# A recurrent kernel on TensorE: input and output projections as three float32r products of halves in place of six bf16 products, with the work of the steps rearranged

## What is computed

```python
# layer 0: a modulated linear layer; ys, d depend on cond only
ys = cond * scale
d = rsqrt(einsum('bi,io->bo', ys * ys, weight * weight) + EPS)
x = x + einsum('bsi,io->bso', x * ys[:, None, :], weight) * d[:, None, :]
# layer 1: a recurrent layer of 256 hidden units over the 256 steps, h0 = cond
Xz, Xr, Xh = X @ Wxz.T + bxz, X @ Wxr.T + bxr, X @ Wxh.T + bxh
def step(H, xs):
    xz, xr, xh = xs
    Z = sigmoid(xz + H @ Whz.T + bhz)
    R = sigmoid(xr + H @ Whr.T + bhr)
    H_tilda = tanh(xh + R * H @ Whh.T + bhh)
    H_new = Z * H + (1.0 - Z) * H_tilda
    return H_new, H_new @ Whq.T + bhq
x = x + scan(step, h0, ...)
```

## Time and profile before

| what | us |
| --- | --- |
| median of 3 runs | 640.48 (639.31 to 640.96) |
| the profiled execution | 639.56 |
| its span, first to last instruction | 637.8 |
| outside its span | 1.76 |
| start of step 0 | 22.5 |

### The profile page before, as it was taken

The page is one execution under the profiler, slowest core; times in us unless marked ns, Lnnn a source line. Parts: engine busy times, 40 slices in busy tenths (PEclk is TensorE's granted clock), DMA queues, the critical chain, the costliest instruction groups (busy, mean ns, idle before and its releaser), DMA issues.

```text
span 637.8 us, 39807 instructions
## 1 busy us (share of the span) xinstructions
PE 626.3 (98%) x16890; PEld 568.1 (89%) x16890; DVE 491.6 (77%) x4051; ACT 209.1 (33%) x1607; POOL 4.5 (1%) x11
## 2 busy tenths in 40 slices
PE   8999999999999999999999999999999999999987
PEld 3689999999999999999999999999999999999976
DVE  5789777777877778777877877777777777877776
ACT  3133333333233333333333333333333333333332
POOL 2000000000000000000000000000000000000000
PEclk9955555555555555555555555555555555555555
DMA  7000000000000000000000000000000000000000
GB/s 264 2 5 3 4 13 4 13 4 12 4 5 12 5 12 4 12 5 4 13 4 13 4 5 12 5 12 5 12 5 4 12 4 13 4 13 4 4 12 12
DMA packets 7174, 8.86 MB, mean 14 GB/s; under 512 B 1618, under 2 KB 5458, under 8 KB 6996
## 3 DMA queue, kind: packets, MB, share of 16 engines
q1 hardware_dynamic: 6416, 6.03, 2.9%
q10 hardware_dynamic: 580, 0.28, 0.2%
HBM read 4.21 MB, written 2.10 MB: 10 GB/s over the span
## 4 chain that ended last, share of the span: by engine, by line
PE 93%; DVE 4%; ACT 1%; DMA 1%; issue 1%; DVEq 0%
PE chunk_bank L670 53%; PE z_rec_bank L670 13%; PE chunk_bank L647 12%; PE y_bank L632 6%; PE z_bank L647 6%; PE chunk_bank L679 1%; DMA x<-x_cm 1%; PE chunk_bank L584 1%; DVE lin L383 1%; DVE r_hidden L517 1%; DVE hidden L563 1%; DVE r_hidden L521 0%; DVE r_hidden L525 0%; ACT scan_mul L327 0%; DVE xs L376 0%
## 5 line engine op out<-in xcount | busy, mean ns | idle before, releaser
L670 PE MATMUL chunk_bank<-r_hidden,w_part 128*128 128x8 bf16 x6144 | 206.2, 169 | 0.2
L670 PEld LDWEIGHTS chunk_bank<-r_hidden,w_part 128*128 128x128 bf16 x6144 | 184.7, 105 | 17.9 <-issue 0.6
L670 PEld LDWEIGHTS chunk_bank<-hidden,w_part 128*128 128x128 bf16 x3072 | 102.5, 104 | 34.5 <-DVE hidden L563 6.2
L670 PE MATMUL chunk_bank<-hidden,w_part 128*128 128x8 bf16 x3072 | 125.1, 173 | 4.5 <-DVE hidden L563 4.0
L563 DVE TENSOR_TENSOR_SCAN hidden<-scan_mul,hidden 128x24 f32<-128x24 f32 x512 | 80.7, 199 | 60.0 <-ACT hidden L330 53.8
L327 ACT ACTIVATE scan_mul<-z_pre 128x16 f32<-128x16 f32 x256 | 57.2, 223 | 197.1 <-DVE z_pre L529 197.1
L670 PE MATMUL z_rec_bank<-hidden_parts,w_part 128*128 128x24 bf16 x3072 | 121.5, 181 | 0.1
L670 PE MATMUL chunk_bank<-hidden_parts,w_part 128*128 128x8 bf16 x3072 | 119.3, 168 | 0.0
L325 ACT ACTIVATE r_bank<-chunk_bank 128x8 f32<-128x8 f32 x256 | 41.5, 162 | 212.1 <-PE chunk_bank L670 206.6
L670 PEld LDWEIGHTS z_rec_bank<-hidden_parts,w_part 128*128 128x128 bf16 x3072 | 103.2, 104 | 0.2 <-DVE z_rec_bank L465 0.2
L670 PEld LDWEIGHTS chunk_bank<-hidden_parts,w_part 128*128 128x128 bf16 x3072 | 102.9, 104 | 0.0
(11 more groups left out here) (86 smaller groups left out, 667.3 us busy)
## 6 DMA issues: line engine op xcount, KB each, us to landing
x<-x_cm SPq DMA_DIRECT2D x4, 512.0 KB, 7.9
out_cm<-result SPq DMA_DIRECT2D x15, 128.0 KB, 2.1
w_rec<-w_rec_cm SPq DMA_DIRECT2D x1, 768.0 KB, 8.2
w_in<-w_in_cm SPq DMA_DIRECT2D x1, 768.0 KB, 9.8
w_mod<-w_mod_cm ACTq DMA_DIRECT2D x1, 256.0 KB, 5.7
w_out<-w_out_cm SPq DMA_DIRECT2D x1, 256.0 KB, 10.3
out_cm<-result SPq DMA_DIRECT2D x1, 64.0 KB, 2.9
out_cm<-result SPq DMA_DIRECT2D x2, 32.0 KB, 1.9
```

The source lines that it names most:

```text
L670: return nc.tensor.matmul(cols, w_part[wp][:, gate, k, m * P:(m + 1) * P], moving, start=first, stop=True, skip_group_check=True)
```

## The change

- The input projections of blocks 2 to 15 and the output projections of blocks 1 to 14, six bf16 products per tile pair before, become three products of float32r operands (`HALVES`): high half of the weights by high half of the data, low by high, high by low. One is issued in the first slot, two in the second. A float32r tile has 4 bytes an element; a VectorE copy to it makes the high half, and a subtraction the low half.
- x1 (128 columns per block and chunk), the input weights, the output weights and now also the hidden states of a block (`h_hi`, `h_lo`, new) are split in this way. The copy stands where a subtraction stood; the halves of the hidden states are new instructions in steps 0 to 3 of blocks 2 to 15, after `z_pre`. The output weights' bf16 parts, which the products at the end still use, are split in block 2, steps 8 to 11.
- The order within a block: from block 1 on the input projection for Z is in steps 0 to 3, the output projection in steps 4 to 7, R and G stay in 8 to 11 and 12 to 15. Accordingly the single f32 products of block 1 stand in steps 4 to 7, the Z bias (`take_z`) in steps 4 and 5, `finish` in 8 and 9, and the bank that R's second half is written to follows.

```diff
-        x1_rest, x1_rest2 = (sb(name, [P, 2, KC, BC]) for name in ("x1_rest", "x1_rest2"))
-        w_in, w_in_rest, w_in_rest2 = (sb(name, [P, 3, KC, C]) for name in ("w_in", "w_in_rest", "w_in_rest2"))
+        x1_hi, x1_lo = (sb(name, [P, 2, KC, BC], fp32r) for name in ("x1_hi", "x1_lo"))
+        h_hi, h_lo = (sb(name, [P, KC, BC], fp32r) for name in ("h_hi", "h_lo"))
+        w_in = sb("w_in", [P, 3, KC, C])
+        w_in_hi, w_in_lo = (sb(name, [P, 3, KC, C], fp32r) for name in ("w_in_hi", "w_in_lo"))
+        w_out_hi, w_out_lo = (sb(name, [P, KC, C], fp32r) for name in ("w_out_hi", "w_out_lo"))
...
-            return n == 0 or (n == 1 and j < 4)
+            return n == 0 or (n == 1 and 4 <= j < 8)
...
+            def first_x1_half(n, k):
+                nc.vector.tensor_copy(x1_hi[:, n % 2, k, :], x1[:, k, n * BC:(n + 1) * BC]).then_inc(x1_hi_ready, 1)
+            def second_x1_half(n, k):
+                dve.wait_ge(x1_hi_ready, KC * (n - 2) + k + 1)
+                nc.vector.tensor_tensor(x1_lo[:, n % 2, k, :], x1[:, k, n * BC:(n + 1) * BC],
+                                        x1_hi[:, n % 2, k, :].bitcast(fp32), ALU.subtract).then_inc(x1_parts, 1)
...
+            def first_h_half(n, k):
+                nc.vector.tensor_copy(h_hi[:, k, :].rearrange("p (s b) -> p s b", b=B), steps_of_h(k, n)
+                                      ).then_inc(h_hi_ready, 1)
+            def second_h_half(n, k):
+                dve.wait_ge(h_hi_ready, KC * (n - 1) + k + 1)
+                nc.vector.tensor_tensor(
+                    h_lo[:, k, :].rearrange("p (s b) -> p s b", b=B), steps_of_h(k, n),
+                    h_hi[:, k, :].bitcast(fp32).rearrange("p (s b) -> p s b", b=B), ALU.subtract
+                ).then_inc(h_halves, 1)
...
+                if n == 2 and 8 <= j < 12:
+                    weight_split(j % 2, 1 + (j - 8) // 2)
...
-                if n > 0 and j in (4, 5):
-                    finish(n - 1, j - 4)
+                if n > 1 and j < 4:
+                    (first_h_half, second_h_half)[j % 2](n - 1, j // 2)
+                if n > 0 and j in (8, 9):
+                    finish(n - 1, j - 8)
...
+            HALVES = ((0, 0), (1, 0), (0, 1))
+            SLOTS_OF = (slice(0, 1), slice(1, len(HALVES)))
...
+                    for i in range(len(HALVES))[SLOTS_OF[slot]]:
+                        wp, part = HALVES[i]
+                        mm = nc.tensor.matmul(pre(1 - p, task, m, 0, BLOCK), (w_in_hi, w_in_lo)[wp][:, task, k, cols],
+                                              (x1_hi, x1_lo)[part][:, (n + 1) % 2, k, :], start=(j == 0 and i == 0),
+                                              stop=True, skip_group_check=True)
...
-                bulk(n, j, slice(0, 1))
+                bulk(n, j, 0)
...
-                bulk(n, j, slice(1, len(PRODUCTS)))
+                bulk(n, j, 1)
```

More of the change, by code:

```diff
@@ L43, in modulated_linear_then_gru @@
     bf16 = mybir.dt.bfloat16
+    fp32r = mybir.dt.float32r
     ALU = mybir.AluOpType
@@ L159, in r_gate @@
         def r_gate(k, n, j):
-            bank = r_bank if k == 0 else (z_bank if n > 0 and j < 4 else y_bank)
+            bank = r_bank if k == 0 else (z_bank if n > 0 and 4 <= j < 8 else y_bank)
             return bank[:, KC * BC:KC * BC + B]
@@ L195, in modulated_linear_then_gru @@
         weight_parts = sem("weight_parts")
-        x1_rest_ready = sem("x1_rest_ready")
+        x1_hi_ready = sem("x1_hi_ready")
         x1_parts = sem("x1_parts")
+        h_hi_ready = sem("h_hi_ready")
+        h_halves = sem("h_halves")
+        weight_hi = sem("weight_hi")
+        weight_halves = sem("weight_halves")
         gates_seeded = sem("gates_seeded")
@@ L397, in take_z, with steps_of_h @@
                                         z_bank[:, m * BC:(m + 1) * BC], bias_z[:, m:m + 1], None, ALU.add)
[L399 to L409, removed]
+            def first_x1_half(n, k):
[4 more added lines that the diff above has]
+                                        x1_hi[:, n % 2, k, :].bitcast(fp32), ALU.subtract).then_inc(x1_parts, 1)
+            def steps_of_h(k, n):
+                return h_word(k, slice(n % 2 * BLOCK, (n % 2 + 1) * BLOCK))
+            def first_h_half(n, k):
[7 more added lines that the diff above has]
+                ).then_inc(h_halves, 1)
             def add_x(k, cols):
@@ L471, in _, with weight_halves_of, weight_split @@
             dve.wait_ge(scan_set, 1)
-            def weight_split(i, part):
-                w, rest, rest2 = (w_in, w_in_rest, w_in_rest2) if i < 3 * KC else (w_out, w_out_rest, w_out_rest2)
+            def weight_halves_of(i, part):
+                w, hi, lo = (w_in, w_in_hi, w_in_lo) if i < 3 * KC else (w_out, w_out_hi, w_out_lo)
                 at = (i // KC, i % KC) if i < 3 * KC else (i - 3 * KC,)
-                w, rest, rest2 = (a[(slice(None),) + at + (slice(None),)] for a in (w, rest, rest2))
+                w, hi, lo = (a[(slice(None),) + at + (slice(None),)] for a in (w, hi, lo))
+                if part == 1:
+                    nc.vector.tensor_copy(hi, w).then_inc(weight_hi, 1)
+                else:
+                    dve.wait_ge(weight_hi, i + 1)
+                    nc.vector.tensor_tensor(lo, w, hi.bitcast(fp32), ALU.subtract).then_inc(weight_halves, 1)
+            def weight_split(k, part):
+                w, rest, rest2 = (a[:, k, :] for a in (w_out, w_out_rest, w_out_rest2))
                 if part == 1:
@@ L480, in weight_split @@
                 else:
-                    dve.wait_ge(weight_rest, i + 1)
+                    dve.wait_ge(weight_rest, k + 1)
                     nc.vector.tensor_tensor(rest2, rest, high(rest), ALU.subtract).then_inc(weight_parts, 1)
@@ L509, in _ @@
                         dve.wait_ge(ld_win, 16)
-                    weight_split((j - 4) % 6, 1 + (j - 4) // 6)
+                    weight_halves_of((j - 4) % 6, 1 + (j - 4) // 6)
                 if n == 1 and 4 <= j < 8:
@@ L513, in _ @@
                         dve.wait_ge(ld_wout, 16)
-                    weight_split(6 + j % 2, 1 + (j - 4) // 2)
+                    weight_halves_of(6 + j % 2, 1 + (j - 4) // 2)
+                if n == 2 and 8 <= j < 12:
+                    weight_split(j % 2, 1 + (j - 8) // 2)
                 for k in range(KC):
@@ L532, in _ @@
                     axis=mybir.AxisListType.X, op=ALU.add).then_inc(pre_z, 1)
-                if n > 0 and j in (4, 5):
-                    finish(n - 1, j - 4)
-                if n + 1 < NB and j in (8, 9):
-                    if j == 8:
+                if n > 1 and j < 4:
+                    (first_h_half, second_h_half)[j % 2](n - 1, j // 2)
+                if n > 0 and j in (8, 9):
+                    finish(n - 1, j - 8)
+                z_at = 8 if n == 0 else 4
+                if n + 1 < NB and j in (z_at, z_at + 1):
+                    if j == z_at:
                         dve.wait_ge(z_ready, n + 1)
-                    take_z(1 - p, j - 8)
+                    take_z(1 - p, j - z_at)
                 if n == LAST and j in (14, 15):
@@ L556, in _ @@
                             dve.wait_ge(x1_ready, x1_count(n + 2))
-                        first_x1_rest(n + 2, j - 12)
+                        first_x1_half(n + 2, j - 12)
                     if j in (14, 15):
-                        second_x1_rest(n + 2, j - 14)
+                        second_x1_half(n + 2, j - 14)
                 for k in range(KC):
@@ L595, in _, with bulk @@
             PRODUCTS = ((0, 0), (1, 0), (2, 0), (0, 1), (1, 1), (0, 2))
-            W_IN = [high(w[:, :, :, :]) for w in (w_in, w_in_rest, w_in_rest2)]
             W_OUT = [high(w[:, :, :]) for w in (w_out, w_out_rest, w_out_rest2)]
[L599 to L605, removed]
+            HALVES = ((0, 0), (1, 0), (0, 1))
+            SLOTS_OF = (slice(0, 1), slice(1, len(HALVES)))
+            def bulk(n, j, slot):
                 p = n % 2
@@ L609, in bulk @@
                 cols = slice(m * P, (m + 1) * P)
-                last = some.stop == len(PRODUCTS)
+                if n == 0:
+                    task = (None, Z, R, G)[j // 4]
+                else:
+                    task = (Z, "out", R, G)[j // 4]
                 if whole_bulk(n, j):
-                    if last and j >= 4:
+                    if slot == 1 and task == "out":
+                        if j == 4:
+                            pe.wait_ge(ld_wout, 16)
+                        mm = out_tile(1 - p, m, k)
+                        if j == 7:
+                            mm.then_inc(y_ready, 1)
+                    elif slot == 1 and task is not None:
                         if j == 4:
@@ L616, in bulk @@
                             pe.wait_ge(gates_seeded, 2 * KC * (n + 2))
-                        mm = in_tile(n + 1, 1 - p, (Z, R, G)[j // 4 - 1], m, k)
+                        mm = in_tile(n + 1, 1 - p, task, m, k)
                         if j == 7:
                             mm.then_inc(z_ready, 1)
```

(35 more changed lines are left out.)

## The result

The changed kernel takes 673.1 us (median of 4 runs, 672.18 to 675.86) against 640.72 (median of 4): a ratio of 1.0513, with a 95% interval of 1.0491 to 1.0536. It is slower by 32 us where 13 were forecast. Direction and place were right, the size was not.

A forecast was written before the change was run, and what follows sets the result against it. The prediction took TensorE's list and the equally long hidden-state path as bounds. Only the first slot cost: 0.06 x 224 = 13.4 us on 639.56 gave 653.0, with 0.9 for the median 654; range 646 to 675 (chance 0.46).

The forecast's parts named there:

- What bounds the kernel: In a loop step, TensorE's list and the hidden-state path over ScalarE and VectorE are equally long, 2.37 us; fewer products gain 0.
- The second slot costs nothing: Between G and the next R: two float32r products need 0.38 of 0.56 us, cost 0.
- The first slot is late and shifts everything behind it: Between Z and G: one float32r product needs 0.19 us of 0.13, so G and the step come 0.06 later, 13.4 us.
- G to R: Sign in the profile after: G start to next R start stays unchanged at 1.22 us.
- The size of the load: Weight load of a float32r product in the loop: 189 ns against 104 for bf16, 0.085 us more, not hidden.
- the agreement with the fast-load rule: For f32 weight loads, the 85 ns between load rows were said to agree with no fast load for fp32.
- The second reading of the same number: Block 1's f32 product: 0.60 us less four column runs, 0.43, leaves 0.17, read as two loads of 0.085 each.
- The spare of the first window: Between Z and G: 0.47 less 0.34 for Z's products leaves 0.13 us, 0.02 to spare beyond a bf16 product.
- the forecast's 0.03 to 0.15: Lateness per step from the first slot's load, from partly hidden to one twice as much too long: 646 to 675 us.
- VectorE: right in cost: New hidden-state halves on VectorE, 56 instructions between `z_pre` and the scan, are covered: cost 0.
- the 16 forecast: VectorE's busy time grows by some 16 us, with no new wait.
- the moved steps: New order within a block: TensorE's new waits are each met at least a scan earlier; no cost was added to the sum.

The follow-up runs named there:

- second_only_clean: Changed kernel without the first slot's float32r product in the 224 steps, that slot's waits moved to the second slot: 640.85 us.
- no_bulk: Changed kernel with all projection products of the 224 steps left out of both slots, the waits moved to the second slot: 643.96 us.
- first_only: Changed kernel with the second slot's two float32r products left out in the 224 steps: 672.29 us.
- narrow_first: Changed kernel with the first slot's float32r product cut to its first 16 columns: 656.64 us.
- the dense stream: Changed kernel with 128 float32r products (32 of 512 columns, 48 of 128, 48 of 8) added behind its last product: 693.96 us.
- bf16_twice: Kernel before with the first slot's bf16 product issued twice: 651.24 us.
- order_bf16: Kernel before with only the order within a block changed, the six bf16 products kept: 639.91 us beside 639.75.
- second_only: Changed kernel with the first slot's float32r product left out in the 224 steps, that slot's waits left where they were: 648.25 us.
- three_second: Changed kernel with all three float32r products in the second slot, none in the first, the first slot's waits left in place: 683.59 us.
- three_second_clean: Changed kernel with all three float32r products in the second slot and the first slot's waits moved there too: 678.89 us.

## Why the prediction was right about the place and wrong about the size

**What bounds the kernel: right.** Taking work off TensorE's list won nothing: 2.37 per step with bf16 products, with two float32r products in the second slot (second_only_clean) and with none (no_bulk, steps 12 to 15).

**The second slot costs nothing: right.** first_only has it empty and takes as long as the changed kernel.

**The first slot is late and shifts everything behind it: right in mechanism.** Both second_only_clean and narrow_first show it. One sign was off: G to R did not stay at 1.22, since part of the lateness lies behind G's first product.

**The size of the load: this step failed.** The forecast put "189 ns against 104 for bf16, 0.085 more" into the sum. The 189 stands in a stage where the clock was granted in full, and the loop runs at half. The table by windows of the kernel before (columns as above) shows it, the last products of layer 0 first, then the f32 steps of block 1:

```profile
22.50:27.50 5.00, 4.88 (x56) 2.77 (x56) 2.11 (x13) 0.46 (x3) 0.00 (x0) 1.00 0.02 5
...
66.80:73.90 7.10, 7.06 (x187) 6.63 (x186) 4.98 (x45) 2.25 (x18) 0.00 (x0) 0.50 0.01 2
```

The pace of float32r loads goes with that clock (0.112 and 0.213), and the records of f32 loads do too (about 190 ns in the first stage, 290 to 333 in the second). The bf16 record hardly differs (96 and 104 ns). On one level of the clock the records are 190 ns against 96, on the other 290 to 333 against 104; the forecast's 85 ns are the difference of two levels, and so is the agreement with the fast-load rule that it saw in them. The right row was in the trace, in the groups by form of the kernel before, and had been passed over:

```profile
L590 PEld LDWEIGHTS y_bank<-hidden_parts,w_out 128*128 128x128 f32 x8 | 2.0, 312 | 0.0
```

With the measured load, the first product should hold TensorE 0.213 longer than the bf16 one did. The timelines say the same without the dense stream. From Z's start to the end of G's row it is 1.27 with one bf16 product between them (302.36 to 303.63), 1.31 with two (bf16_twice, 313.00 to 314.31) and 1.42 with the float32r product (313.73 to 315.15). So the float32r product lasts 0.11 longer than two bf16 products, and 0.11 + 0.107, about 0.22, longer than one. Its whole load sticks out. 0.213 less the 0.065 to spare is 0.148 a step and 33 us, against 0.147 and 32 measured.

**The second reading of the same number was no independent proof.** The forecast split the 0.17 that an f32 product shows beyond its four runs into two loads of 0.085. By the measured load it is rather one load of 0.21, partly overlapped, and a second one hidden behind 0.213 of columns. That this split equalled 189 - 104 was chance, and it closed the question too early.

**The spare of the first window: too small by 0.045.** It was read from starts alone, with 0.34 for Z's products, although the first slot's product starts 0.32 after Z (302.36 and 302.68). Another 0.02 lies behind G's start: where G waits for `r_hidden`, its second product follows at 0.046, and the later ones at 0.027. This error worked against the other one. With the right load and a window of 0.13, the sum would have been 0.19 a step, 43 us; with the right spare and a load of 0.085, it would have been 0.02 a step, 4 us. The measured 0.147 lies inside the forecast's 0.03 to 0.15 only at its edge.

The Trainium skill ("TensorE: Matmul & The Clock Gate", LDWEIGHTS) gives a load's time as its columns over 1.2 GHz; for 128 columns that is an estimate of 107 ns. For float32r the trace agrees at the upper level of the clock (112) and not at the lower (213). The Trainium skill's rule that the fast load is on for 128 weights unless the input type is FP32 (same page, Weight-path perf modes) would, by the letter, give float32r the fast load. The pace of 0.112 at best, where bf16 products follow one another at 0.028 even on the lower level, shows that it has none here.

**VectorE: right in cost.** The copies took 216 ns, the subtractions 280, and they cost nothing: second_only_clean makes all of them and has steps of 2.37. The busy time grew by 7.0 us and not by the 16 forecast. order_bf16 settles the moved steps.

No version here beats the kernel before. The step is held at 2.37 by the path over ScalarE and VectorE, and projection work in any form only has to fit into the two windows.

## What to carry to other kernels

Take a duration only from a stretch with the same granted clock as the place where it will be used; one group by form can hold both (the f32 loads of L584 took 192 to 333 ns, with a mean of 252). Count weight loads and not products when moving operands are short: what matters in a window is how much of the loads is hidden. Before making work cheaper, look for a step that does without it; if that step is no shorter, the change has nothing to win there and can still lose.

## What the runs showed of the hardware

- A float32r product is one record and runs its columns once: 512 columns at 0.43 us on the 1.2 GHz level. Its weight load takes 0.213 us there and 0.112 on the 2.4 GHz level. With 8 or 128 columns on the upper level, the load sets the pace.
- In the dense stream the clock fell back from 1.00 to 0.50 while 8-column products followed one another without a gap: TensorE was busy all the time in the row, and the level was still taken away.
- Two waits in a row ahead of a product, the first for something long done, cost 0.07 a step when the second is the one that holds: 2.44 against 2.37 in second_only, 2.61 against 2.54 in three_second, whose blocks 2 to 14, with 65 such steps, take 4.7 us more than those of three_second_clean. With a product between the two waits, as in the changed kernel, these steps are no longer than the others. What in the issue of the waits takes the time was not tried.
